# A feed-forward layer rewritten group by group: where the gated product is read from, and which engine rounds

## The reference

```
def fp4_quant_dequant(x):            # blocks of 16 along the last dimension
    scale = max(max(abs(xb)) / 6.0, 1e-12)
    xn = xb / scale
    q = GRID[searchsorted(MID, abs(xn))] * sign(xn) * scale   # grid 0 .5 1 1.5 2 3 4 6
def fp4_linear(x, w):
    return einsum(fp4_quant_dequant(x), fp4_quant_dequant(w))
gate = fp4_linear(x, w_gate)         # 128 -> 352
y = fp4_linear(x, w_up)              # 128 -> 352
h = silu(gate) * y
return fp4_linear(h, w_down)         # 352 -> 128
# used as  x = x + 0.5 * ffn(layernorm(x))
```

## Time and profile before

| what | value |
| --- | --- |
| median of 3 runs | 820.65 us (819.05 to 822.27) |
| profiled execution, its own time | 819.17 us |
| span of the profiled execution | 817.5 us |
| mean granted clock of PE over the span | 0.932 |
| busy, PE / DVE / ACT / POOL | 682.5 / 632.0 / 473.4 / 239.5 us |
| ffn_a: first product of silu and up to the last write-back | 427.2 to 545.0 us |
| ffn_b: the same | 696.8 to 814.6 us |

### The profile page before, as it was taken

How to read it: one execution, slowest core, us unless ns; L and a number is a source line. 1 busy time by engine, 2 the same in 40 slices (tenths; PEclk the granted TensorE clock), 3 DMA queues, 4 the chain that set the end, 5 groups by cost and what they waited for, 6 DMA issues and landing times.

```text
span 817.5 us, 16964 instructions
## 1 busy us (share of the span) xinstructions
PE 682.5 (83%) x5826; PEld 492.9 (60%) x5826; DVE 632.0 (77%) x1594; ACT 473.4 (58%) x915; POOL 239.5 (29%) x375
## 2 busy tenths in 40 slices
PE   5999999789988799999957788838898873787885
PEld 3777767577777667777734465534645652455654
DVE  2887888456655668878969999846999975899993
ACT  3877786664663078777755566526454214575652
POOL 5011020456455000110013543011643442345400
PEclk9999999699999699999978999978999995899997
DMA  8000000000000000000000000000000000000000
GB/s 210 2 0 0 0 1 1 2 3 4 0 1 4 2 1 0 0 0 1 0 1 0 1 0 0 0 0 2 1 0 0 0 1 0 1 26 13 23 16 26
DMA packets 13454, 7.00 MB, mean 9 GB/s; under 512 B 1176, under 2 KB 13408, under 8 KB 13408
## 3 DMA queue, kind: packets, MB, share of 16 engines
q1 hardware_dynamic: 11328, 5.33, 2.5%
q10 hardware_dynamic: 2080, 1.05, 0.5%
HBM read 4.28 MB, written 2.10 MB: 8 GB/s over the span
## 4 chain that ended last, share of the span: by engine, by line
PE 45%; DVE 36%; issue 10%; ACT 5%; POOL 2%; DVEq 1%; DMA 0%; ACTq 0%; POOLq 0%
PE ps L1250 41%; DVE ffn_work L786 4%; DVE shared L1046 3%; DVE shared L1074 3%; DVE x_sb L888 3%; DVE fq_h_max L753 2%; DVE ffn_work L1162 2%; DVE ffn_work L791 2%; DVE hq L797 2%; DVE picked L976 2%; DVE stats L822 2%; PE ps L1572 2%; ACT ffn_work L440 2%; ACT xn L470 2%; DVE ffn_work L780 1%
## 5 line engine op out<-in xcount | busy, mean ns | idle before, releaser
L1250 PEld LDWEIGHTS ps<-w_sb,sq_h 128*128 128x128 f32 x1024 | 131.4, 191 | 70.2 <-ACT sq_h L492 51.7
L888 DVE SCALAR_TENSOR_TENSOR x_sb<-ps,gates,x_sb 128x128 f32 (+1 forms) x512 | 147.1, 343 | 22.5 <-PE ps L1250 18.7
L1250 PE MATMUL ps<-w_sb,sq_h 128*128 128x128 f32 x1024 | 137.7, 277 | 1.5 <-ACT sq_h L492 1.4
L1250 PE MATMUL ps<-xnT,w_sb 128*128 128x512 f32 x256 | 135.2, 612 | 0.0
L310 POOL TENSOR_SCALAR vareps<-meanvar 128x4 f32<-128x4 f32 (+1 forms) x44 | 22.5, 511 | 354.3 <-DVE meanvar L831 338.3
L488 ACT ACTIVATE relu_h<-ps 128x512 f32<-128x512 f32 x128 | 75.7, 592 | 59.5 <-PE ps L1250 59.2
L470 ACT ACTIVATE xn<-x_sb,shift,rstd 128x128 f32 (+1 forms) x192 | 79.7, 481 | 17.6 <-POOL shift L318 17.6
L492 ACT ACTIVATE sq_h<-relu_h 128x512 f32<-128x512 f32 x128 | 80.6, 630 | 4.1
L676 ACT ACTIVATE hqT<-ps 128x384 f32<-128x384 f32 x64 | 30.0, 489 | 67.4 <-PE ps L1572 66.5
L1250 PE MATMUL ps<-gateT,xnT 128*128 128x352 f32 x128 | 56.8, 528 | 14.2 <-ACT ffn_work L670 10.7
L1250 PE MATMUL ps<-downT,hqT 128*128 128x128 f32 x384 | 62.7, 306 | 3.2 <-ACT hqT L676 3.0
(11 more groups left out here) (156 smaller groups left out, 1265.5 us busy)
## 6 DMA issues: line engine op xcount, KB each, us to landing
x_sb<-in_L_attn_x_dram SPq DMA_DIRECT2D x8, 256.0 KB, 6.9
out_dram<-x_sb SPq DMA_DIRECT2D x8, 256.0 KB, 2.3
w_sb<-in_L_ffn_w_all_dram ACTq DMA_DIRECT2D x2, 512.0 KB, 6.1
wraw<-in_L_attn_qkv_w_dram SPq DMA_DIRECT2D x1, 192.0 KB, 4.9
wraw<-attn_in_proj_weight_dram SPq DMA_DIRECT2D x1, 192.0 KB, 4.1
fraw<-in_L_ffn_w_down_dram SPq DMA_DIRECT2D x1, 176.0 KB, 2.8
fraw<-in_L_ffn_w_gate_dram SPq DMA_DIRECT2D x1, 128.0 KB, 2.8
fraw<-in_L_ffn_w_up_dram SPq DMA_DIRECT2D x1, 128.0 KB, 2.5
```

Source lines behind the costliest of these rows:

```text
L888: t = nc.vector.scalar_tensor_tensor(tile_b(i, j), bank(4 + e % 4, TPB, C)[:, j, :], gates[:, j, e:e + 1], tile_b(i, j), ALU.mult, ALU.add)
L1250: return nc.tensor.matmul(o, a, b, start=start, stop=stop, **kw)
```

## The change

Both feed-forward phases are written out for all 8 groups on every engine, with fixed addresses and no loops. In them:

- "up" stays in PSUM. Its four tiles get a bank each (2 to 5), the copies of line 672 go, and DVE's product reads the four banks at once. "Gate" keeps one bank (1) where it had two; each gate matmul waits for the silu before it. The transposed h takes banks 6 and 0, and x's transposes, which also write bank 0, wait for the fourth copy of h.
- h is written with a stride of 17, and a constant 6e-12 stands behind each block of 16, so that the maximum already has its floor. The scale pass of h goes: the division multiplies by 6 and by the reciprocal of the maximum in one `scalar_tensor_tensor`, and the last product multiplies by the maximum itself. The factor 1/6 moves into the down weights.
- The last product of h is split: DVE writes the first two tiles (`hq_ready`), POOL the other two (`hq_late`), which PE awaits before the third tile's transposes and DVE before the next division.
- x's rounding offset is made by ACT in two passes, a Square and an Identity with a bias, for x of groups 2 to 7. DVE adds it to x in one `tensor_tensor`; POOL takes it off again and multiplies by the scale (`x_back`).
- ACT writes group g-1 back after the magnitude of h of group g, not at the end of group g-1.
- Four semaphores that only mark passed points become one; this touches the other phases in name alone.

```diff
 # POOL
-            def x_rescale(s, i):
-                pool.wait_ge(s["tr_done"], i)
-                pool.wait_ge(s["hid_done"], i)
-                nc.gpsimd.tensor_tensor(xblocks[1], vblocks, per_block(fq_x[3]), ALU.mult).then_inc(s["xq_ready"], 1)
+                def h_late(g):
+                    pool.wait_ge(s["hq_ready"], g + 1)
+                    nc.gpsimd.tensor_tensor(hq_blocks(EARLY, TPB - EARLY), by_block(fq_h[0], EARLY, TPB - EARLY),
+                                            late(h_max[:, g % 2, :]), ALU.mult).then_inc(s["hq_late"], 1)
+                def x_back(g):
+                    pool.wait_ge(s["x_snapped"], g - 1)
+                    ch.link(nc.gpsimd.tensor_tensor(v, m, v, ALU.subtract))
+                    pool.wait_ge(s["tr_done"], g)
+                    nc.gpsimd.tensor_tensor(quantized, vb, per_block(fq_x[3]), ALU.mult).then_inc(s["xq_ready"], 1)
+                for g in range(GROUPS):
+                    if g > 0:
+                        h_late(g - 1)
+                    if 2 <= g + 1 < GROUPS:
+                        x_back(g + 1)
+                    if g + 2 < GROUPS:
+                        x_divide(g + 2)
+                    if g + 3 < GROUPS:
+                        layer_norm(g + 3)
+                h_late(GROUPS - 1)
 # ACT
-                nc.scalar.activation(downT[:, :, :], bank(5, 3, P), ACT.Copy, scale=-0.5 * (1.0 - NUDGE)).then_inc(s_prep_act, 1)
+                nc.scalar.activation(downT[:, :, :], bank(5, 3, P), ACT.Copy, scale=-0.5 / 6.0).then_inc(s_prep_act, 1)
-                    nc.scalar.activation(silu_g[:, j, :], bank(1 + j % 2, FI), ACT.Silu).then_inc(s["silu_ready"], 1)
-                    act.wait_ge(s["up_done"], i * TPB + j + 1)
-                    nc.scalar.activation(up_sb[:, j, :], bank(3 + j % 2, FI), ACT.Copy).then_inc(s["up_ready"], 1)
+                    nc.scalar.activation(silu_g[:, j, :], bank(1, FI), ACT.Silu).then_inc(s["silu_ready"], 1)
+                def x_binades(g):
+                    act.wait_ge(s["x_divided"], g + 1)
+                    nc.scalar.activation(fq_x[1], fq_x[0], ACT.Square, scale=CURVE).then_inc(s["x_sized"], 1)
+                    act.wait_ge(s["x_sized"], 2 * g - 1)
+                    nc.scalar.activation(fq_x[1], fq_x[1], ACT.Identity, bias=m_base[:, 0:1]).then_inc(s["x_sized"], 1)
+                def body(g):
+                    act.wait_ge(s["h_divided"], g + 1)
+                    magnitude(fq_h[0], fq_h[1]).then_inc(s["h_sized"], 1)
+                    if g > 0:
+                        x_out(g - 1)
+                    if g + 1 < GROUPS:
+                        silu(g + 1, 0)
+                        silu(g + 1, 1)
+                    if g + 2 < GROUPS:
+                        x_binades(g + 2)
+                    if g + 1 < GROUPS:
+                        silu(g + 1, 2)
+                        silu(g + 1, 3)
+                    hidden_T(g, 0)
+                    hidden_T(g, 1)
+                    if g + 3 < GROUPS:
+                        normal(g + 3)
+                    hidden_T(g, 2)
+                    hidden_T(g, 3)
+                    if g + 2 < GROUPS:
+                        evac_xnT(s, g + 2)
 # DVE
+                    nc.vector.tensor_tensor(h3.rearrange("p (j k) w -> p j k w", k=KB),
+                                            silu_g[:, :, :].rearrange("p j (k w) -> p j k w", w=BLK),
+                                            ps[:, 2:6, 0:FI].rearrange("p j (k w) -> p j k w", w=BLK),
+                                            ALU.mult).then_inc(s["hid_done"], 1)
+                    dve.wait_ge(s["hid_done"], g + 1)
+                    ch.link(nc.vector.tensor_reduce(largest, hid[:, :, :], AX, ALU.max, apply_absolute_value=True))
+                    ch.link(nc.vector.reciprocal(h_inv[:, :], largest))
+                    if g > 0:
+                        dve.wait_ge(s["hq_late"], g)
+                    nc.vector.scalar_tensor_tensor(blocks(v), h3, 6.0 * (1.0 - NUDGE),
+                                                   h_inv[:, :].unsqueeze(2).to_broadcast([P, NBH, BLK]),
+                                                   ALU.mult, ALU.mult).then_inc(s["h_divided"], 1)
...
-                    h4.snap()
-                    h4.unbias()
-                    if ahead:
-                        x4.snap()
-                    h4.rescale()
-                    if ahead:
-                        x4.unbias()
+                    dve.wait_ge(s["h_sized"], g + 1)
+                    snapped = ch.add(nc.vector.scalar_tensor_tensor(v, m, MAGIC, v, ALU.max, ALU.add))
+                    ch.need(snapped)
+                    unbiased = ch.add(nc.vector.scalar_tensor_tensor(v, m, MAGIC, v, ALU.max, ALU.subtract))
+                    if g + 2 < GROUPS:
+                        dve.wait_ge(s["x_sized"], 2 * (g + 2))
+                        nc.vector.tensor_tensor(fq_x[0], fq_x[1], fq_x[0], ALU.add).then_inc(s["x_snapped"], 1)
+                    ch.need(unbiased)
+                    nc.vector.tensor_tensor(hq_blocks(0, EARLY), by_block(v, 0, EARLY), early(largest),
+                                            ALU.mult).then_inc(s["hq_ready"], 1)
 # PE
-                        if j >= 2:
-                            pe.wait_ge(s["silu_ready"], i * TPB + j - 1)
-                        mm(bank(1 + j % 2, FI), tok(j), gateT[:, 0:FI]).then_inc(s["gate_done"], 1)
-                        if j >= 2:
-                            pe.wait_ge(s["up_ready"], i * TPB + j - 1)
-                        mm(bank(3 + j % 2, FI), tok(j), upT[:, 0:FI]).then_inc(s["up_done"], 1)
+                        if g * TPB + j > 0:
+                            pe.wait_ge(s["silu_ready"], g * TPB + j)
+                        mm(bank(1, FI), tok(j), gateT[:, 0:FI]).then_inc(s["gate_done"], 1)
+                        if g > 0 and j == 0:
+                            pe.wait_ge(s["hid_done"], g)
+                        mm(bank(2 + j, FI), tok(j), upT[:, 0:FI]).then_inc(s["up_done"], 1)
```

More of the change, by code:

```diff
@@ L37 @@
 BLK = 16
+NBH = 4 * FI // BLK
+KB = FI // BLK
+EARLY = 2
 LN_EPS = 1e-5
@@ L170, in macaron @@
         fq_x = fq_bufs("fq_x", 5 * TPB * FI, TPB * C)
-        silu_g, up_sb, hid = [work(k * TPB * FI, TPB * FI).rearrange("p (j f) -> p j f", j=TPB) for k in (2, 3, 4)]
+        silu_g = work(2 * TPB * FI, TPB * FI).rearrange("p (j f) -> p j f", j=TPB)
+        hid = work(3 * TPB * FI, NBH * (BLK + 1)).rearrange("p (k w) -> p k w", w=BLK + 1)
+        h_max = sb("h_max", [P, 2, NBH])
+        m_base = sb("m_base", [P, 1])
         relu_q = work(0, T)
@@ new lines, in normal, with x_magnitude @@
+                def normal(g):
+                    act.wait_ge(s["rstd_ready"], g + 1)
+                    into = TPB if g == 1 else 0
+                    for j in range(TPB):
+                        a = nc.scalar.activation(xn[:, into + j, :], tile_f(g, j), ACT.Identity,
+                                                 scale=rstd[:, j:j + 1], bias=shift[:, j:j + 1])
+                    a.then_inc(s["xn_ready"], 1)
+                def x_magnitude(g):
+                    act.wait_ge(s["x_divided"], g + 1)
+                    magnitude(fq_x[0], fq_x[1]).then_inc(s["x_sized"], 1)
@@ L711, in ffn @@
                 for j in range(TPB):
-                    silu_up(0, j)
+                    silu(0, j)
                 evac_xnT(s, 1)
-                with act.Fori(0, GROUPS - 3) as i:
-                    body(i, True, False, True)
-                body(GROUPS - 3, True, False, False)
-                body(GROUPS - 2, False, False, False)
-                body(GROUPS - 1, False, True, False)
+                for g in range(GROUPS):
+                    body(g)
+                x_out(GROUPS - 1)
             moe(S["moe_a"], S["linatt"], True)
@@ L1175, in body @@
                         x4.largest()
-                        dve.wait_ge(s["xq_ready"], i + 2)
+                        dve.wait_ge(s["xq_ready"], g + 2)
                         x4.nudged_scales()
                         x4.inverse_out(s["x_inverse"])
-                    if further:
-                        moments(halves(i + 3))
-                    h4.snap()
-                    h4.unbias()
-                    if ahead:
-                        x4.snap()
-                    h4.rescale()
@@ L1194, in ffn @@
                 dve.wait_ge(s["xn_ready"], 2)
-                moments(halves(2))
+                moments(2)
                 x_alone(1)
-                pre = ch.k
-                with dve.Fori(0, GROUPS - 3) as i:
-                    ch.start(i * PER["ffn"] + pre)
-                    body(i, True, True)
-                    assert ch.k == PER["ffn"], ("ffn", ch.k)
-                ch.start((GROUPS - 3) * PER["ffn"] + pre)
-                body(GROUPS - 3, True, False)
-                body(GROUPS - 2, False, False)
-                body(GROUPS - 1, False, False)
+                for g in range(GROUPS):
+                    body(g)
```

(35 more changed lines are left out.)

202 lines of the change are left out of this document (96 added, 106 removed).

## The result

The changed kernel takes 807.95 us (median of 4 runs, 805.28 to 809.21); the kernel before, on the same chip, 820.32 (819.05 to 822.27). The ratio is 0.984, with a 95% interval of 0.982 to 0.986: 1.6% faster, where 811.8 us was forecast. The profiled execution took 808.67 us with a span of 806.6, 10.9 less than before's 817.5.

The account below looks back on a forecast made before the run. DVE was taken to bound the feed-forward groups; 14.0 + 5 x 12.95 + 12.7 + 11.45 = 102.9 for 109.86 a phase, +2.5 at the start, gives -8.9 in all: 811.8 us, range 803 to 820.

Parts of the forecast that it names:

- rival 1: DVE alone bounds, the clock stays high and POOL's passes miss the division: 8.5 us less a phase, 803.7 us; chance 0.17.
- DVE's list: DVE's instructions in one group of four tiles, end to end: 14.20 us cut to 12.70 by shorter or moved passes.
- The chain over ACT and PE: Magnitude, write-back, then silus and single-bank gates in 1.42 us steps: next product at H + 12.65, H being this product's start.
- The third chain: Hidden transposes to x's next copy, 5.42 us: ACT free for the next magnitude at about H + 5.9, against 5.8 wanted.
- POOL: Its three passes end 0.23 us after the division should start, so the division waits: inner groups 12.95 us.
- The start of the phase: Serial silus and a low clock delay the first product by 1.2 to 4.1 us; 2.5 taken.
- Group 0: First group of a phase: 12.7 us at full clock, 15.2 at half; 14.0 taken.
- Group 6: Next-to-last group, without x passes: 7.6 + 0.2 + 4.9 = 12.7 us, more than in the kernel before.
- Rival 2: POOL runs its half of h in 1.75 us, division 0.58 late, groups 13.3: 815.3 us in all; chance 0.12.
- rival 3: The low clock takes both starts and both first groups whole, +1.6 + 1.2 us a phase: 817.4 us; chance 0.10.
- Rival 4: Single gate bank at low clock inside the phase, 3.8 us a group; five such groups give 831 us; chance 0.08.
- Rival 5: Square is not in silu's table: two loads of 1.28 us a group on ACT, 843 us; chance 0.03.

Follow-up runs that it names:

- e3: The changed kernel with the last product of h whole on DVE again, POOL's half gone: 815.81 us, ratio 0.993 to the kernel before.
- e4: The changed kernel with the subtraction of x's rounding offset back on DVE, behind the half product of h: 812.90 us, ratio 0.990.
- e7: The changed kernel with one more 512-element ACT copy ahead of x's offset passes: 812.11 us, ratio 0.990.
- e8: The same extra 512-element ACT copy as in e7, added to e1, the kernel with two gate banks: 796.00 us, ratio 0.970.
- e1: The changed kernel with gate in two banks (1 and 6), so PE runs one pair ahead of the silus: 796.33 us, ratio 0.970.
- e5: The changed kernel with an extra 256-element POOL product into a spare tile ahead of x's product: 810.65 us, ratio 0.988.
- e6: The changed kernel with unread matmuls in PE's pauses, one before group 0's second gate, five before group 1's: 803.23 us, ratio 0.979.
- e2: The kernel before with only the loops of both feed-forward phases written out: 820.86 us, ratio 0.9997.

## Why the prediction came out as it did

The forecast was 811.8 us and the time is 807.95, about halfway to rival 1's 803.7; the number alone would not tell the two apart. Two of the signs named for the forecast case did not come: the inner groups are 12.70 and not 12.9 to 13.0 apart, and no division is lengthened by 0.2.

**DVE's list: right.** 12.70 forecast, 12.70 found; e3 and e4 show that DVE's share passes into the groups in full.

**The chain over ACT and PE: right.** First silu at H + 7.66 for H + 7.6, steps of 1.42, last "up" at H + 12.67 for H + 12.65. e7 shows it without slack and e8 shows that the single bank is the reason. That the four removed "up" copies bring nothing in the inner groups fits e1, which frees 2 us of this chain while the groups stay; no run puts the copies back.

**The third chain: right.** The magnitude started at H + 5.92 for 5.9, behind the copy of x and 0.15 after the division ended.

**POOL: mechanism right, size off.** The step was "0.23 too late. The division waits, and both chains become 12.94". h took 1.39 for 1.4 and the subtraction 1.28 for 1.27. But POOL started at H + 0.41, not 0.5, and the starts of its passes stand 1.35 and 1.36 apart where 1.4 and 1.35 were reckoned, and the product took 1.06 for 1.12, so the last ends at H + 4.18 for the 4.37 forecast: 0.04 late and not 0.23. And some 0.15 of an overlap cost nothing (e5: 0.47 lost of 0.62). So the groups are 12.70, not 12.95: 5 x 0.25 = 1.25 a phase, 2.5 in all. In the inner groups that is rival 1's case; the reasoning about the two engines holds, as e5 shows where POOL is 0.62 late.

**The start of the phase: right within its estimate.** +2.5 taken, +2.75 and +2.52 found. e6 splits the first into 1.14 of serial silus (1.2 forecast) and 1.61 of low clock. The step between two silus at the low clock was 429.59 - 427.24 = 2.35 for the 2.34 estimated. How many of the three steps would be slow was not worked out: the 2.5 was picked between 1.2 and 4.1, and that it lies so close is luck.

**Group 0: too dear.** 14.0 taken between 12.7 and 15.2, 13.51 and 13.45 found: the second and third gate took 1.54 and 1.38 to their ends and the fourth 0.82, so the low clock covered two of the four pairs, and the group lies a third of the way between the bounds. 0.5 a phase.

**Group 6: too dear by 0.32.** Forecast 7.6 + 0.2 + 4.9 = 12.7. Found: first silu at H + 7.56, three steps of 1.40 to 1.42, and the product 4.82 behind the first silu, 12.38. The 0.2, set aside for a wait that no row showed, did not come. Group 7: 11.45, found 11.41.

**"No loops" for nothing: right.** e2: 0.9997.

**The sum.** Forecast -4.45 a phase, found -6.30 (9.05 less 2.75), or -6.56 in the second phase. The difference of 1.9 is 1.25 of POOL, 0.5 of group 0, 0.32 of group 6 and 0.04 of group 7, less 0.25 at the start. Over both phases that is 4.0 us, and the median measured is 3.9 below the 811.8 forecast. The chains stand as forecast; what did not come is POOL's lateness and the wait set aside in group 6.

**Rivals.** Rival 1 (no lateness of POOL) was right for the inner groups and wrong for the clock. Rival 2 (h at 1.75) is refuted by 1.39, rival 3 (low clock takes the starts and group 0 whole) by 6.44 and 13.51. Rival 4 (low clock in the inner groups) did not come: PE was granted 0.98 from 440 to 520, and from 703 to 783 in the second phase. Rival 5 (Square needs a table load) did not come: the table of single lines has two loads at silu's line, one at the head of each phase (its columns are least, median and most duration, and first and last start), and Square's line has none.

```profile
L735 ACT ACT_TABLE_LOAD  x2: 1283/1283/1283, 423.9 to 687.4; - x2
```

## What to carry to other kernels

When a change frees time on the bound engine, write down the next chain's length in the same units: here three chains ended within 0.1 us of each other, so small additions to any one of them (0.62 on ACT, 0.62 on POOL, 0.6 on DVE) came through to three quarters or more (0.52, 0.46, 0.60). A buffer given up to save copies may cost nothing in the steady state and all its price at the edges: one PSUM bank more for "gate" brought 11.6 us, about as much as the whole change, some 10 of it at the start, in group 0 and in group 6, and none in the inner groups. Where PE pauses for some microseconds ahead of a serial chain, look at the granted clock; matmuls that compute nothing shortened the run by 4.7 us. And before a difference of 1 or 2 us is given to an edit, see how far stretches of the same code spread: the tail took 6.7 to 8.1 us in the kernels with one gate bank.

## What was not expected of the hardware

- DVE's wait for POOL shows as a longer instruction, 2.10 for 1.63 us, with no idle time and no releaser in its row; POOL's own pass beside it kept its 1.06. Of an overlap of 0.62 us 0.47 was lost, of one of 0.04 nothing.
- Beside DVE's passes with two SBUF inputs, POOL's four-element instructions took 1.33 to 1.57 us, three in a row, as here in the changed kernel (POOL in order of time). At their shortest in the same run they took 0.23, 0.23 and 1.04. They are not free: POOL's half of h stands behind them and starts at H + 0.41, though DVE has written its own half by H + 0.08. Here that uses up the room ahead of the division, whose start POOL's last pass overruns by 0.04:

```profile
478.82 1.49 POOL L407 TENSOR_SCALAR vareps<-meanvar 128x4 f32<-128x4 f32 x1
480.39 1.57 POOL L408 TENSOR_SCALAR negmean<-meanvar 128x4 f32<-128x4 f32 x1
482.05 1.33 POOL L409 TENSOR_TENSOR rstd<-vareps,minus_half 128x4 f32<-128x4 f32 x1
```
- ACT's Square ran between silus 12 times without a table load.
- The same code between the two phases took 146.9 to 149.1 us with mean clocks of 0.91 to 0.88, a spread that no edit here explains.
